# Attention with 11 probability buffers, visits of four key tiles, row sums grown in place by GpSimd and DMA, and gate weights loaded late

## The reference

```
xn = layernorm(x)                                  # x: 2 x 2048 x 1024, fp32
q, k, v = xn @ wq, xn @ wk, xn @ wv                # 32 query heads, 8 key/value heads of 32
scores  = causal(q k^T / sqrt(32)); attn = softmax(scores)
s = (attn @ v) @ wo
g = silu(xn @ W_base.T + b_base + lora_out)        # lora: top 2 of 8 experts, rank 16
out = x + s * g
```

## Time and profile before

| | us |
|---|---|
| runs, median of 3 | 3545.49 (3539.39 to 3545.74) |
| the profiled execution's own time | 3544.42 |
| its span, first to last instruction | 3542.6 |
| TensorE busy | 3360.0 |
| VectorE, ScalarE, GpSimd busy | 1873.0, 1435.3, 1291.0 |
| mean granted TensorE clock | 0.975 |

### The profile page before, as it was taken

The page is one execution under the profiler, slowest core; times in us unless marked ns, Lnnn a source line. Parts: engine busy times, 40 slices in busy tenths (PEclk is TensorE's granted clock), DMA queues, the critical chain, the costliest instruction groups (busy, mean ns, idle before and its releaser), DMA issues. The chain is left out here.

```text
span 3542.6 us, 63490 instructions
## 1 busy us (share of the span) xinstructions
PE 3360.0 (95%) x19200; PEld 2236.6 (63%) x19200; DVE 1873.0 (53%) x4613; ACT 1435.3 (41%) x2658; POOL 1291.0 (36%) x446
## 2 busy tenths in 40 slices
PE   6999999799999999999999999999999799989999
PEld 5888888555555555555555555555554588878887
DVE  5333332567667677667666676677763122223333
ACT  3222221155555556556555565566666110110000
POOL 0000000156666576565565575566667000000000
PEclk9999999699999999999999999999999899999999
DMA  6555544534534444444444444453533444445555
GB/s 224 158 160 179 170 155 133 147 82 106 126 97 112 114 102 108 109 102 116 101 108 115 96 117 110 98 126 98 120 88 93 135 160 144 141 132 178 190 192 175
DMA packets 278980, 461.98 MB, mean 130 GB/s; under 512 B 40352, under 2 KB 156064, under 8 KB 262816
## 3 DMA queue, kind: packets, MB, share of 16 engines
q1 hardware_dynamic: 258960, 328.32, 31.1%
q0 software_dynamic: 16128, 117.45, 14.3%
q10 hardware_dynamic: 3600, 12.58, 1.1%
HBM read 205.03 MB, written 134.74 MB: 96 GB/s over the span
## 5 line engine op out<-in xcount | busy, mean ns | idle before, releaser
L1030 ACT ACTIVATE probs<-cols_ps 128x512 f32<-128x512 f32 x2176 | 1148.8, 611 | 577.5 <-PE cols_ps L977 471.9
L1053 DVE TENSOR_REDUCE row_max<-rows_ps 128x1 f32<-128x512 f32 x1536 | 992.9, 681 | 374.3 <-PE rows_ps L894 372.8
L977 PE MATMUL cols_ps<-q_st,k_st 97*128 97x512 f32 x2176 | 909.3, 427 | 52.3 <-ACT probs L1030 36.3
L894 PE MATMUL rows_ps<-k_st,q_st 96*128 96x512 f32 (+3 forms) x2560 | 900.1, 381 | 28.6 <-DMA q_st<-scratch_q_hi 17.2
L859 POOL TENSOR_TENSOR added<-added,probs 128x2048 f32<-128x2048 f32 x192 | 898.8, 4681 | 26.9 <-ACT probs L1030 21.1
L977 PEld LDWEIGHTS cols_ps<-q_st,k_st 97*128 97x128 f32 x2176 | 412.6, 190 | 399.1 <-issue 221.6
L1057 DVE CUSTOM_DVE_ANT_0 masked_rows<-rows_ps,tri 128x128 bf16<-128x128 f32 (+3 forms) x1024 | 485.9, 484 | 237.2 <-PE rows_ps L894 233.8
L894 PEld LDWEIGHTS rows_ps<-k_st,q_st 96*128 96x128 f32 x2560 | 496.0, 194 | 167.2 <-DVE row_max L1053 69.7
L932 PE MATMUL o_ps<-probs,v_st 128*32 128x512 f32 (+3 forms) x5120 | 539.6, 540 | 2.6 <-ACT probs L1030 2.6
L859 POOL TENSOR_TENSOR added<-probs 128x2048 f32<-128x2048 f32 x48 | 220.0, 4583 | 629.8 <-PE cols_ps L977 614.6
L932 PEld LDWEIGHTS o_ps<-probs,v_st 128*32 128x32 f32 x5120 | 134.9, 110 | 269.1 <-issue 202.4
(11 more groups left out here) (105 smaller groups left out, 3150.4 us busy)
## 6 DMA issues: line engine op xcount, KB each, us to landing
dma_added<-probs POOLq DMA_DIRECT2D x112, 1024.0 KB, 6.9
q_st<-scratch_q_hi SPq DMA_DIRECT2D x128, 256.0 KB, 5.3
x_sb<-in_x SPq DMA_DIRECT2D x32, 512.0 KB, 4.0
scratch_xt_hi<-xt_hi SPq DMA_DIRECT2D x32, 512.0 KB, 6.0
scratch_xt_lo<-xt_lo SPq DMA_DIRECT2D x32, 512.0 KB, 6.8
scratch_q_hi<-out_hi SPq DMA_DIRECT2D x64, 256.0 KB, 2.5
scratch_q_lo<-out_lo SPq DMA_DIRECT2D x64, 256.0 KB, 2.9
q_st<-scratch_q_lo SPq DMA_DIRECT2D x64, 256.0 KB, 4.7
```

The costliest lines, as they stand in the source:

```text
L894: nc.tensor.matmul(rows_ps[rows_slot(k)][:, 0:keys], q_st[c][0:K1, h, i * P:(i + 1) * P], k_st[kbuf][0:K1, CH * p:CH * p + keys], start=Tr ...
L977: ins = nc.tensor.matmul(into, k_st[n.u][:, j * P:(j + 1) * P], q_st[c][:, :, i * P:(i + 1) * P], start=True, stop=not diagonal)
L1030: nc.scalar.activation(probs_of(c, j)[:, :, i * P:(i + 1) * P], cols_ps[cols_slot(AT_T[t])][:, :].rearrange("p (h q) -> p h q", h=NREP), A ...
L1053: nc.vector.tensor_reduce(into, bank[:, :], AX.X, ALU.max).then_inc(rows_free, 1)
```

## The change

1. **Visits.** `PER_VISIT = [2, 4, 4, 4]`: chunk 0 keeps visits of two key tiles, the others take four in one visit: 2, 2, 3 and 4 visits. A visit is due 2 tiles behind its last key tile's last score tile: (0,0) behind tile 9, (0,2) 12, (1,0) 28, (1,4) 38, (2,0) 54, (2,4) 70, (2,8) 80, (3,0) 96, (3,4) 112, (3,8) 128, (3,12) 138.
2. **Sums.** Chunk c's sum "Y" moves directly ahead of visit (c+1, 0): behind tiles 28, 54, 96, and 145 (tile 9 of the next group). It is made of `added[c % 2]` and `dma_added[c % 2]` alone; `REST` is gone. There are two buffers of each kind.
3. **Growing in place.** The exponential writes key tile 0 of a chunk (and 1, in chunks 1 to 3) straight into `added` (`dma_added`), and visits read them there. Everything else is added to them: 3, 4, 7 and 9 adds on GpSimd, 0, 2, 3 and 5 accumulating DMAs, no plain copy. The first add and the first DMA of a chunk wait for its first visit (`values_done`), later DMAs for the DMA before them, as they did. GpSimd's queue for chunk 3 from tile 96 on: add 3, DMA 2, DMA 4 (97), add 5 (101), 6 (105), DMA 7 (109), add 8 (113), the normalization of chunk 2 (115), DMA 9 (117), add 10 (121), DMA 11 (125), adds 12, 13, 14, 15 (129 to 135). Chunk 2 from tile 54: add 3, DMA 2, DMA 4 (55), adds 5, 6 (59, 63), DMA 7 (67), add 8 (71), the normalization of chunk 1 (73), adds 9, 10, 11 (74 to 77). Chunk 1 from tile 28: add 3, DMA 2, DMA 4 (29), adds 5, 6, 7 (32 to 35).
4. **Buffers.** 11 probability buffers in a ring of the 33 key tiles of a group that are not written in place.
5. **Peel.** `PEEL = 3`: the loop's turn lies at the start of chunk 3 of every second group.
6. **Gate weights.** The nine slices are loaded raw during the last group by SP, over query and key buffers that are no longer needed, and both halves are made at the start of the gate stage by ScalarE and VectorE; TensorE's first gate tile takes the slices k in turn, for both halves of the output, behind each low half.
7. ScalarE's copy "O" waits for the store of the chunk two before, and the store of the inverses has a semaphore for each buffer.

```
-NROWS, NCOLS, NPROBS = 4, 3, 6
+NROWS, NCOLS, NPROBS = 4, 3, 11
-NVG = NJG // 2
+PER_VISIT = [2, 4, 4, 4]
+V_OFF = [sum(TPC * (cc + 1) // PER_VISIT[cc] for cc in range(c)) for c in range(CPB + 1)]
+NVG = V_OFF[CPB]
-ADDS = [[], [0, 1, 2, 3], [0, 1, 3, 5, 6, 8], [0, 1, 3, 4, 6, 7, 9, 11]]
-DMA_ADDS = [[], [], [2, 4, 7], [2, 5, 8, 10]]
-REST = [[j for j in range(TPC * (c + 1)) if j not in ADDS[c] + DMA_ADDS[c]] for c in range(CPB)]
+ADDS = [[0, 1, 2, 3], [0, 3, 5, 6, 7], [0, 3, 5, 6, 8, 9, 10, 11], [0, 3, 5, 6, 8, 10, 12, 13, 14, 15]]
+DMA_ADDS = [[], [1, 2, 4], [1, 2, 4, 7], [1, 2, 4, 7, 9, 11]]
+RING = [(c, j) for c in range(CPB) for j in range(TPC * (c + 1)) if j not in ADDS[c][:1] + DMA_ADDS[c][:1]]
...
+def weighed_at(c, j):
+    return tiles_through(c, j - j % PER_VISIT[c] + PER_VISIT[c] - 1) + VISIT_AFTER - 1
+
 for _c in range(CPB):
-    for _j in range(0, TPC * (_c + 1), 2):
-        _t = tiles_through(_c, _j + 1) + VISIT_AFTER - 1
-        event(_t, "W", _c, _j)
+    _t = weighed_at((_c + 1) % CPB, 0) + (0 if _c + 1 < CPB else NTG)
     event(_t, "Y", _c)
-    event(_t + 2, "O", _c)
...
+for _c in range(CPB):
+    for _j in range(0, TPC * (_c + 1), PER_VISIT[_c]):
+        event(weighed_at(_c, _j), "W", _c, _j)
+    event(weighed_at(_c, _j) + 2, "O", _c)
+    for _list, _kind in ((ADDS, "A"), (DMA_ADDS, "D")):
+        for _j in _list[_c][1:]:
+            event(max(tiles_through(_c, _j) - 1, weighed_at(_c, _list[_c][0])), _kind, _c, _j)
...
-        PEEL = 2
+        PEEL = 3
...
         def probs_of(c, j):
-            return probs[probs_slot(J_OFF[c] + j)]
+            if j in ADDS[c][:1]:
+                return added[c % 2]
+            if j in DMA_ADDS[c][:1]:
+                return dma_added[c % 2]
+            return probs[probs_slot(RING.index((c, j)))]
...
             def add(n, c, back, j):
+                total = added[c % 2]
                 pool.wait_ge(probs_ready, made_count(n, c, back, j))
+                if j == ADDS[c][1]:
+                    pool.wait_ge(values_done, weighed_count(n, c, back, ADDS[c][0]))
                 else:
                     pool.wait_ge(pool_added, n.lin(NADD, adds_through(c, j) - 1))
...
             def dma_add(n, c, back, j):
                 wait_apart(pool, probs_ready, made_count(n, c, back, j), passed_pool)
+                if j == DMA_ADDS[c][1]:
+                    wait_apart(pool, values_done, weighed_count(n, c, back, DMA_ADDS[c][0]), passed_pool)
                 else:
                     wait_apart(pool, dma_done, n.lin(16 * NDMA, 16 * (dma_adds_through(c, j) - 1)), passed_pool)
+                pool.dma_start(dma_added[c % 2][:, :, q0:CH], probs_of(c, j)[:, :, q0:CH], accum_op=ALU.add).then_inc(dma_done, 16)
...
             def row_sums(n, cc, back):
-                parts = [(probs_of(cc, j), max(0, j - TPC * cc) * P) for j in REST[cc]]
+                pe.wait_ge(pool_added, n.lin(NADD, adds_through(cc, NJG) - back * NADD))
+                parts = [added[cc % 2]]
                 if DMA_ADDS[cc]:
                     pe.wait_ge(dma_done, n.lin(16 * NDMA, 16 * (dma_adds_through(cc, NJG) - back * NDMA)))
+                    parts.append(dma_added[cc % 2])
...
 def gate(...):                                    # ScalarE, VectorE, TensorE
+            for k in range(NW):
+                nc.scalar.activation(w_hi[:, k, :], w_raw[:, k, :], ACT.Copy).then_inc(w_hi_ready, 1)
+            for k in range(NW):
+                dve.wait_ge(w_hi_ready, k + 1)
+                nc.vector.tensor_sub(w_lo[:, k, :], w_raw[:, k, :], w_hi[:, k, :].bitcast(FP32)) \
+                    .then_inc(w_lo_ready, 1)
+            for k in range(NW):
+                pe.wait_ge(w_lo_ready, k + 1)
+                for half in range(2):
+                    ins = step(0, half, k)
```

More of the change, by code:

```diff
@@ L618 @@
 NADD = sum(len(a) - 1 for a in ADDS if a)
-NDMA = sum(map(len, DMA_ADDS))
+NDMA = sum(len(a) - 1 for a in DMA_ADDS if a)
 def adds_through(c, j):
@@ L627, in dma_adds_through, with attend @@
 def dma_adds_through(c, j):
[L629 to L632 removed]
+    return sum(max(0, len(a) - 1) for a in DMA_ADDS[:c]) + sum(1 for t in DMA_ADDS[c][1:] if t <= j)
+def attend(nc, sc, ident, ident_r, mask_ji, tri, wb, lb):
     ctx = ExitStack()
@@ L643, in attend @@
         NL = NREP * CH // P
-        q_st = [sb(f"q_st{i}", [K1 + 1, NREP, CH], FP32R) for i in range(CPB)]
-        k_st = [sb(f"k_st{i}", [K1 + 1, S], FP32R) for i in range(2)]
+        with nc.sbuf_tensor("gw_raw", [P, KT + 1, D], FP32) as gw_raw:
+            pass
+        q_st = [sb(f"q_st{i}", [K1 + 1, NREP, CH], FP32R) for i in range(CPB - 1)]
+        k_st = [sb("k_st0", [K1 + 1, S], FP32R)]
+        sb("gw_raw_end", [P, D])
+        q_st.append(sb("q_st_last", [K1 + 1, NREP, CH], FP32R))
+        k_st.append(sb("k_st1", [K1 + 1, S], FP32R))
         v_st = [sb(f"v_st{i}", [P, S // P, HD]) for i in range(2)]
@@ L683, in attend @@
         l_inv_ready = sem("a_l_inv_ready")
-        l_inv_stored = sem("a_l_inv_stored")
+        l_inv_stored = [sem(f"a_l_inv_stored{i}") for i in range(2)]
         l_spread = [sem(f"a_l_spread{i}") for i in range(2)]
@@ L687, in attend @@
         o_stored = [sem(f"a_o_stored{i}") for i in range(2)]
-        gw_loaded = [sem(f"a_gw_loaded{i}") for i in range(2)]
-        gw_hi_ready = sem("a_gw_hi_ready")
-        gw_lo_ready = sem("a_gw_lo_ready")
+        gw_loaded = sem("a_gw_loaded")
         NW = KT + 1
@@ L741, in cols_free_count, with weighed_count @@
             return None if first_group(n) and before < 0 else cols_count(n, before)
[L743 to L747, removed]
+        def weighed_count(n, c, back, j):
+            return n.lin(NVG, visit_of(c, j) + 1 - back * NVG)
         def rows_count(n, ahead, k):
@@ L806, in run @@
                             load_q(n.lin(1, 0 if c == 0 else 1), (c - 1) % CPB)
-                    elif kind == "K" and not last_group:
+                        else:
+                            load_gw(2 * c - 2)
+                            load_gw(2 * c - 1)
+                    elif kind == "K":
                         if not isinstance(n.pair, int) or n.pair > 0 or n.u > 0:
                             wait_apart(sp, values_done, n.lin(NVG, 0), passed)
-                        load_kv(n.lin(1, 1), 1 - n.u)
+                        if last_group:
+                            for k in range(2 * CPB - 2, NW):
+                                load_gw(k)
+                        else:
+                            load_kv(n.lin(1, 1), 1 - n.u)
                     elif kind == "M":
@@ L927, in weigh @@
                         pe.wait_ge(v_loaded[vbuf], n.pair * 16 + 16)
-                pe.wait_ge(probs_ready, made_count(n, cc, back, j0 + 1))
-                for j in (j0, j0 + 1):
+                pe.wait_ge(probs_ready, made_count(n, cc, back, j0 + PER_VISIT[cc] - 1))
+                for j in range(j0, j0 + PER_VISIT[cc]):
                     q0 = max(0, j - TPC * cc) * P
@@ L1101, in _, with gate @@
             over_stages(dve, run)
-def gate(nc, b_base, sc, w_hi, w_lo, wo, ow_hi, ow_lo):
+        return gw_raw
+def gate(nc, b_base, sc, w_raw, wo, ow_hi, ow_lo):
     ctx = ExitStack()
```

140 lines of the change are left out of this document (61 added, 79 removed).

## The result

| | before | after |
|---|---|---|
| median of the runs, us | 3545.61 (3539.39 to 3552.27), 4 runs | 3881.72 (3876.87 to 3883.33), 4 runs |
| ratio after / before, 95% interval | | 1.0945 (1.0923 to 1.0968) |
| span of the profiled execution | 3542.6 | 3878.7 |
| mean granted TensorE clock | 0.975 | 0.923 |

The change costs 336 us, 9.5%. The forecast was 3740, +195: the sign was right, the size was not, and the time lies above the range.

A forecast was written before the change was run, and what follows sets the result against it. TensorE bound the stage before; afterwards GpSimd's chains would: 115.5 us work plus 19.9 waits, with clock losses about 140 a group. Sixteen cycles plus 6 us: 2246 against 2049.5, +197, less 2, giving 3740; range 3590 to 3810.

The forecast's parts named there:

- The mechanism: Attention stage: GpSimd's adds queue behind DMAs awaiting earlier landings, so TensorE waits at sums; cycle 134 to 144 us, chance 0.77.
- The failed term: GpSimd's accumulating DMAs: each lands 7.3 us after its start, the price used for every place in the chains.
- The chains: GpSimd's adds and DMAs from the end of a chunk's first visit: 20.0, 36.0 and 49.3 us for chunks 1 to 3.
- Rival 3: Every accumulating DMA takes 9.6 us, chains 13 us longer a cycle, clock 5 more: 158 a cycle, 4030 us; chance 0.05.
- Chunk 2's chain: GpSimd's adds, DMAs and normalization for chunk 2: 36.0 us against TensorE's 29, so a wait of 7 us.
- the line: GpSimd's narrow adds, interpolated between 1.28 and 4.59 us: 3.5, 2.4 and 1.3 us for widths 384, 256 and 128.
- rival 1: Attention stage: TensorE stays the bound, adds and DMAs hidden; 138 us less, 3405, up to 3500 with VectorE; chance 0.08.
- The waits of TensorE: TensorE at sums 1, 2 and 3 waits 2.6, 7 and 10.3 us for GpSimd, 19.9 a group; none at sum 0.
- The clock: TensorE at half clock behind waits loses 0.5, 2 and 2.5 us after sums 1, 2 and 3.
- The path of 115.5 us: TensorE's work for one attention group in the new order, without waits: 115.5 us.
- The prices of visits and sums: TensorE: 0.23 us for each visit in all, 0.86 for a 512-wide part, 1.27 for the three narrow parts.
- The weights: Nine conversions moved from the attention stage's head to the gate stage: gain 2 us, cost 0, upper bound 3.

The follow-up runs named there:

- Experiment 3: Kernel after with only GpSimd's queue reordered: each chunk's first DMA ahead of its first add, later accumulating DMAs issued behind more adds; 3642.90 us, 1.0276.
- experiment 1: Kernel after with only one add a chunk and one accumulating DMA in chunks 1 to 3, most key tiles missing from the sums; 3413.88 us, 0.963.
- experiment 2: Kernel after with all 23 adds a group but without the accumulating DMAs of key tiles 4, 7, 9 and 11; 3431.20 us, 0.9679.
- experiment 6: Kernel after with SyncE's query, key and value loads of later groups cut to an eighth of their columns; 3839.80 us, 1.0831.
- experiment 4: Kernel after with 20, 16 and 44 dummy matmuls ahead of TensorE's waits at sums 1, 2 and 3; 3868.68 us, 1.0913.
- experiment 5: The kernel of experiment 1 with visits of two key tiles everywhere, sums and chain starts unmoved; 3363.60 us, 0.9495.
- experiment 9: Kernel after, all adds and DMAs kept, with visits of two key tiles everywhere; 3833.50 us, 1.0791.
- Experiment 11: Kernel after with GpSimd's queue reordered, visits of two key tiles, and chunk 3's key tiles 9, 11 and 12 summed by TensorE; 3418.52 us, 0.9617.

## What the prediction had right, and which term failed

- **The mechanism held.** GpSimd's queue stands at DMA 4 (forecast 6.5 us, shown 6.67) with the adds behind it. Experiment 3 shows it by moving the waits alone: -239 us. Experiments 1 and 2 exclude that TensorE's work or the number of adds sets the time.
- **The failed term: 7.3 us from one accumulating DMA to the next.** The chains were forecast 3.9, 0.7 and 3.5 us too short, 8.1 of the 8.7 us by which the cycle missed. Where a DMA waits for the one before it, the chain pays two things, and both were mis-sized: the landing, taken as 7.3 us wherever the DMA stands, and the start of the next DMA behind the landing, taken as nothing. In the kernel after, the next one started 0.57 us behind the landing in 79 of 80 cases (0.566 to 0.583). The kernel before has the same 0.57, and the prediction's own rows show it: the DMA of 1592.58 landed after 7.3 us (its line stands below), and the one that waited for it started at 1600.44, 7.86 us behind its start. In chunk 1 (means of 14 groups) DMA 2 landed after 10.3 us, 3.0 above the price; with the 0.57 that is 3.6 of the 3.9. In chunk 3 three DMAs wait for another (4, 9 and 11): the landings before them, 7.0, 7.7 and 8.8 us, are 1.6 above three times 7.3 together, and the three starts behind them cost 1.7. That is 3.3 of the 3.5.

```profile
DMA to landing us min/median/max: 7.3/7.3/7.3
```

- **Why the landings were long.** With most of SyncE's loads taken away (experiment 6) chunk 1's first landing is 8.0 us and those of chunk 3 are 7.2, 7.6 and 7.6, so 2.3 and 1.1 us of the misses are those loads. What is left above 7.3 is 0.7 us in chunk 1 and 0.5 in chunk 3; chunk 1's landing alternates there from group to group, 8.8 and 7.3 us in the means, from a cause that no run separates. DMA 11's own 12.5 us, the largest of all, cost next to nothing in after, where the adds end as late. In experiment 3, where they don't, it took 13.2 us in the same 14 groups, so some 6 of the 11.7 us of wait are what it took above 7.3, and the other 6 are what was expected. Rival 3 (every landing 9.6) had the direction but put it on every DMA.
- **Chunk 2's chain** was nearly right (36.0, 36.7): one DMA waits there, its landing was 7.2 us, and the 0.57 behind it is most of the difference. Adds 3.49, 2.38 and 1.29 us long at widths of 384, 256 and 128 lay on the line (3.5, 2.4, 1.3), so rival 1's condition of cheaper narrow adds fell.
- **The waits of TensorE** came to 5.6, 4.0 and 12.7 us, 22.3 together (19.9 forecast). Sum 0 never waits, as worked out. In the six of the 14 groups that hold the loop's turn there is no wait at sum 2, in the others it is 6.3 to 7.7 us: the turn was taken in by the wait, as forecast.
- **The clock** was put at 5 us a group. Experiment 4 gives 3.5 on the path. In after 28.5 us of a group run at half clock, and most of it while GpSimd's chain would have been waited for anyway. The term was somewhat high as a sum, and misplaced: from sum 1 to the next chain 7.3 us for 5.9, from sum 2 6.6 for 7.4, and 1.0 behind sum 3 by experiment 4 where 2.5 was put.
- **The path of 115.5 us** was 118.0 without the turn (experiment 1), the 2.5 us in the long stretches. The prices of visits and sums held. What failed is that a visit of four was counted as a pure gain of 2.1 us a group: the hold by VectorE stood only in rival 1, 1 us for each of 6 long visits, and experiment 5 gives 2.1 + 3.1, some 5 us, for all of them together. The forecast's cycle did not turn on it, since in after the chains set the time (there the visits of two bring 48 us, mainly through earlier starts of the chains, experiment 9).
- **The weights** gave what was priced: the fourth score tile of the stage starts at 711.96 us for 714.04, and TensorE's wait before the gate is 21.64 us for 23.68, with 759.7 for 760.7 us behind it.

```profile
3118.96 0.79 PE L1236 MATMUL g_acc<-gw_hi,g_t_hi 128*128 128x512 f32 x1 [21.64 <-DMA g_t_lo<-scratch_hw_lo]
```

- **Rival 1** needed the chains to vanish, and experiment 1 removed them: 3414 where it had 3405. So the 128 us of saved work can be had once no chain is late. Experiment 11 has every key tile in its sums and lies 134 us below the kernel before on its chip: three parts went back to TensorE, 2.6 us a group, and the visits of two, 3.1 us a group in experiment 5, paid for them.

## What to carry to other kernels

Before an engine is given more work because it is idle 64% of the time, walk its queue in order and ask which instruction waits there, and what stands behind it: a wait for a transfer in the queue that also computes costs the computing too, and moving it a few places was worth more here (239 us) than all the work the change saved. Price a transfer at the place where it will run, by what the other queues move there, not at the median of the old places, and read the price of a chained one from start to start, so that the step from one landing to the next start is in it. And longer visits to one kind of work starve the engine that feeds on the other kind: count the bank buffers against the visit's length before counting the switches saved.

## What the runs showed of the hardware

- In the kernel after, an accumulating DMA of 1 MB between two buffers of SBUF took 7.0 to 8.6 us to land in the means of most places, 10.4 at the first place of chunk 1, and 12.5 us (13.3 at most) where SyncE's loads ran with it; with most of the loads cut the last was 7.4. The Trainium skill (DMA: Bandwidth & Descriptors, Anatomy of one DMA) gives a fit from which an estimate of 4.4 us follows for this size; the trace does not agree for an accumulating DMA, the shortest of which took 6.8 us in the runs here.
- A DMA that GpSimd holds back until the one before it has landed starts 0.57 us behind that landing (79 times in after, 16 in the kernel before).
- TensorE at half clock is not by itself lost time. Raising the granted clock from 0.923 to 0.968 (experiment 4) gave 13 of the 336 us, since TensorE was waiting for GpSimd's chains.
- A column-tiled visit of four key tiles in place of two is slower by 3.1 us a group net, although it changes the mode nine times less often in a group (experiment 5 against 1).
